# Top-31 search of a sparse attention layer: the 512 scores of a row searched as 256 pairs

## The reference, cut to what matters

```python
x = x + 0.5 * ffn(layernorm(x), ...)
x = x + attn(layernorm(x), ...)
x = x + 0.5 * ffn(layernorm(x), ...)

def attn(x, Wq, bq, Wk, bk, Wv, bv, Wo, bo):        # 16 heads of 16
    scores = einsum('bhqd,bhkd->bhqk', Q, K) / sqrt(D)          # 512 keys a row
    thresh = lax.top_k(scores, U)[0][..., -1:]                  # U = 31
    scores = where(scores < thresh, -inf, scores)
    context = einsum('bhqk,bhkd->bhqd', softmax(scores), V)
    return context @ Wo.T + bo

def layernorm(x, eps=1e-05):
    m = mean(x); v = var(x)
    return (x - m) / sqrt(v + eps)
```

## Time and profile before

| | us |
|---|---|
| median of 3 runs | 4726.12 |
| lowest and highest of them | 4723.4, 4728.99 |
| span of the profiled execution | 4725.1 |
| DVE busy | 4393.5 (93%) |
| PE busy | 4132.2 (87%) |
| ACT busy | 3967.9 (84%) |
| POOL busy | 2995.0 (63%) |

### The profile page before, as it was taken

The page is one execution under the profiler, slowest core; times in us unless marked ns, Lnnn a source line. Parts: engine busy times, 40 slices in busy tenths (PEclk is TensorE's granted clock), DMA queues, the critical chain, the costliest instruction groups (busy, mean ns, idle before and its releaser), DMA issues. The chain is left out here.

```text
span 4725.1 us, 123794 instructions
## 1 busy us (share of the span) xinstructions
PE 4132.2 (87%) x33100; PEld 3423.4 (72%) x33100; DVE 4393.5 (93%) x10203; ACT 3967.9 (84%) x10181; POOL 2995.0 (63%) x4946
## 2 busy tenths in 40 slices
PE   6778899899999889999998999998899989987777
PEld 5556777777777777777777777777777777765555
DVE  2499999999999999999999999999999999999982
ACT  2488889898898889989888998988899889888772
POOL 1445677677667767766776776677677667654440
PEclk8889999999999999999999999999999999988888
DMA  3111111121111111111111111111111111111011
GB/s 100 45 27 35 49 50 53 50 55 50 52 51 51 53 50 55 50 52 51 51 53 50 55 50 52 51 51 53 50 53 50 54 51 51 51 38 26 22 30 50
DMA packets 244162, 232.66 MB, mean 49 GB/s; under 512 B 27123, under 2 KB 176628, under 8 KB 243316
## 3 DMA queue, kind: packets, MB, share of 16 engines
q1 hardware_dynamic: 243444, 224.49, 16.6%
HBM read 214.98 MB, written 9.44 MB: 47 GB/s over the span
## 5 line engine op out<-in xcount | busy, mean ns | idle before, releaser
L1027 DVE MAX8 M<-W 128x8 f32<-128x512 f32 x2688 | 1735.2, 681 | 57.8 <-DVE W L1029 2.5
L679 PE MATMUL pQ<-wf_sb,HS 128*128 128x192 f32 x8192 | 1545.3, 345 | 81.3 <-POOL HS L419 54.1
L679 PEld LDWEIGHTS pQ<-wf_sb,HS 128*128 128x128 f32 x8192 | 1438.3, 203 | 129.5 <-issue 65.9
L1029 DVE MATCH_REPLACE8 W<-M,W 128x512 f32<-128x512 f32 x1664 | 1115.0, 676 | 0.0
L1072 POOL TENSOR_TENSOR XL<-S,LM 128x512 f32<-128x512 f32 x384 | 445.6, 1160 | 908.4 <-ACT LM L909 895.5
L698 PE MATMUL pST<-ident,S 128*128 128x128 f32 x4096 | 747.9, 283 | 15.4 <-ACT S L897 15.4
L924 ACT ACTIVATE OUT<-S,M 128x512 bf16<-128x512 f32 x1024 | 741.5, 724 | 0.0
L928 ACT ACTIVATE S<-S,M 128x512 f32<-128x512 f32 x1024 | 737.2, 720 | 0.0
L700 PE MATMUL pST<-steep,OUT 128*128 128x128 bf16 x4096 | 731.8, 222 | 0.0
L1029 DVE MATCH_REPLACE8 W<-M,S 128x512 f32<-128x512 f32 x1024 | 684.3, 676 | 0.0
L1027 DVE MAX8 M<-S 128x8 f32<-128x512 f32 x1024 | 651.5, 678 | 20.8 <-ACT S L897 10.7
(11 more groups left out here) (267 smaller groups left out, 6585.2 us busy)
## 6 DMA issues: line engine op xcount, KB each, us to landing
RB<-rows_b SPq DMA_DIRECT2D x384, 256.0 KB, 3.3
RB<-rows_a SPq DMA_DIRECT2D x384, 256.0 KB, 3.3
x_b<-in_x SPq DMA_DIRECT2D x64, 128.0 KB, 2.8
out_y<-y SPq DMA_DIRECT2D x64, 128.0 KB, 1.8
wf_sb<-in_wf SPq DMA_DIRECT2D x4, 768.0 KB, 7.4
rows_b<-rwT_b SPq DMA_DIRECT2D x64, 8.0 KB, 1.3
wof_sb<-in_wof SPq DMA_DIRECT2D x1, 1024.0 KB, 7.1
rows_a<-rwT_a SPq DMA_DIRECT2D x64, 8.0 KB, 1.4
```

The source lines that it names most:

```text
L679: mm = nc.tensor.matmul(pQ[:, 0:QKV], HS[:, k % 2, e, i, :], wf_sb[:, i, at:at + QKV], start=k + e + i == 0, stop=(k, e, i) == (3, 3, 1))
L1027: nc.vector.max(m, src[i]).then_inc(s_tk, 1)
L1029: nc.vector.match_replace(W[:, i, :], m, src[i], -BIG).then_inc(s_tk, 1)
```

## The change

**The search.** The keys are stored so that the scores matmul gives, in the first 256 columns, the difference of the scores of key j and key j + 256, and in the last 256 the score of key j + 256. For that the key tile holds three blocks (`KK`): ACT writes the two halves, POOL writes their difference after each key projection. ACT leaves each unit in three instructions of 256 columns: the second half to S, the positive part and the negative part of the difference to a new tile HL (a ring of 12). POOL adds (larger of the pair, `hi`), and makes by two subtractions the first half of S and the smaller of the pair (`lo`). DVE searches 10 passes: seven over 256 (hi: MAX8, strike, MAX8, strike; lo: MAX8, strike, MAX8, where the 16 largest of lo land beside hi) and three over 272 (hi and these 16: MAX8, strike, MAX8). All units are searched this way. The light units and all of their instructions on ACT and POOL are gone. The search of a pair of units stands two slots later than before; POOL's split stands one slot ahead of it.

**The short steps.** The mean of a layer norm is no longer scaled by a POOL instruction: ACT's square takes the factor. The gate's `RL` and `mk` go, `em` becomes two instructions. The negative maximum of the small attention comes from DVE's reduction. mixT is now written over RB2, whose load waits for the end of the matmuls that read it. Some tiles are shared by both jobs.

```diff
-SC, EV, TOP, OUTS, GAP, TR, PTE, PV, CT, CTT, CTX = 2, 3, 4, 10, 11, 16, 17, 18, 19, 20, 21
-LOW, LCOPY, LTOP, LPICK, LTH = 6, 6, 8, 9, 10
+SC, EV, SPLIT, TOP, OUTS, GAP, TR, PTE, PV, CT, CTT, CTX = 2, 3, 5, 6, 10, 11, 16, 17, 18, 19, 20, 21
...
+STEPS = (HI8, LO8, HIR, LOR, HI16, LO16, HIR2, ALL8, ALLR, ALL16)
+ORDER = [(i, k) for k in STEPS for i in range(2)]
...
-        "pT": 114, "rb2": 110, "attT": 116, "mix": 117, "y": 119, "out": 120,
+        "pT": 114, "rb2": 114, "attT": 116, "mix": 117, "y": 119, "out": 120,
...
-                ns.tensor_tensor(mixT[:], J.attT[:].unsqueeze(1).broadcast_to([P, 8, P]), RB2[:], ALU.mult
+                ns.tensor_tensor(RB2[:], attT[:].unsqueeze(1).broadcast_to([P, 8, P]), RB2[:], ALU.mult
...
-                    nc.tensor.matmul(pST[h][:], QT[r:r + 32, g // 2, g % 2, m * P:(m + 1) * P], KT[r:r + 32, g // 2, :],
+                    nc.tensor.matmul(pST[h][:], QT[r:r + 32, g // 2, g % 2, m * P:(m + 1) * P],
+                                     KK[r:r + 32, g // 2, 1:3, :].rearrange("p a j -> p (a j)"),
...
-                        nc.scalar.copy(S[:, (4 * c + h) % RING, :], pST[h][:]).then_inc(s_ev, 1)
+                        nc.scalar.copy(S[:, u % RING, HALVES:T], pST[h][:, HALVES:T])
+                        nc.scalar.activation(entry[:, 0:HALVES], pST[h][:, 0:HALVES], ACT.Relu)
+                        nc.scalar.activation(entry[:, HIL:HIL + HALVES], pST[h][:, 0:HALVES], ACT.Relu, scale=-1.0
+                                             ).then_inc(s_ev, 1)
...
-                if at := light(w, j, LCOPY):
...
-                    nc.gpsimd.tensor_tensor(XL[:, c % 2, :], S[:, r, :], LM[:, c % 2, :], ALU.subtract).then_inc(s_lx, 1)
+                for c in range(2):
+                    if at := at_proj(f"K{c}", w, j):
+                        pool.wait_ge(jobs["b"].sem["read"], fill("b", w, j) + 1)
+                        nc.gpsimd.tensor_tensor(KK[:, c, 1, :], KK[:, c, 0, :], KK[:, c, 2, :], ALU.subtract
+                                                ).then_inc(s_kd, 1)
+                if at := soon(w, j, "SPLIT", SPLIT, 2, PAIRS * NB):
+                    n, c = at
+                    for u in (2 * c, 2 * c + 1):
+                        entry = HL[:, place(w, u), :]
+                        pool.wait_ge(s_ev, w.count(SPAN, u + 1))
+                        nc.gpsimd.tensor_tensor(entry[:, 0:HALVES], S[:, u % RING, HALVES:T], entry[:, 0:HALVES], ALU.add
+                                                ).then_inc(s_hi, 1)
+                    for u in (2 * c, 2 * c + 1):
+                        entry = HL[:, place(w, u), :]
+                        pool.wait_ge(s_hi, w.count(SPAN, u + 1))
+                        nc.gpsimd.tensor_tensor(S[:, u % RING, 0:HALVES], entry[:, 0:HALVES], entry[:, HIL:HIL + HALVES],
+                                                ALU.subtract)
+                        nc.gpsimd.tensor_tensor(entry[:, HIL:HIL + HALVES], S[:, u % RING, HALVES:T],
+                                                entry[:, HIL:HIL + HALVES], ALU.subtract).then_inc(s_lo, 1)
```

More of the change, by code:

```diff
@@ L144, in earlier, with passed, place @@
     return w.count(k_all, c_all)
-def passed(w, c, k):
-    p, i = c % GANG // 2, c % 2
-    return w.count(SPAN // GANG * len(ORDER), c // GANG * len(ORDER) + ORDER.index((p, i, k)) + 1)
-def light(w, j, slot):
-    for k, u in enumerate(LIGHT):
-        if at := due(w, j, slot + u // 2 * 2, GANG, SPAN // GANG * NB):
-            n, c = at
-            return n * len(LIGHT) + k, c * len(LIGHT) + k, GANG * c + u
-    return None
+def passed(w, u, k):
+    return w.count(SPAN // 2 * len(ORDER), u // 2 * len(ORDER) + ORDER.index((u % 2, k)) + 1)
+def place(w, u):
+    return (SPAN * w.lo + u) % RINGH
 def fill(n, w, j):
@@ L388, in layer @@
                 if ends:
-                    wait(eng, g, 7 * t)
+                    wait(eng, g, 5 * t)
                 eng.wait_ge(q["repl"], t + 1)
@@ L402, in layer @@
                 eng.wait_ge(q["gate_exp"], t + 1)
-                ns.tensor_tensor(J.em[:], J.eg[:], J.mk[:], ALU.mult).then_inc(q["gate_em"], 1)
+                ns.tensor_tensor(J.ep[:], J.eg[:], J.pos[:], ALU.mult).then_inc(q["gate_em"], 1)
+                wait(eng, q["gate"], 5 * t + 5)
+                eng.wait_ge(q["gate_em"], 2 * t + 1)
+                ns.tensor_tensor(J.em[:], J.ep[:], J.fb2[:], ALU.add).then_inc(q["gate_em"], 1)
             if at := mine("rw"):
@@ L511, in ffn @@
                     held(sp, q["rw_st"], 16 * t + 16)
-                    held(sp, s_mix, earlier(w, j, MIXES.values()))
+                    held(sp, s_yd, earlier(w, j, MIXES.values()))
                     pairs = J.rows[c % 2].rearrange("(c o) t -> o c t", o=2)
@@ L623, in ffn @@
                     for k in range(4):
-                        nc.tensor.matmul(F[:, 0:D], mixT[:, k, :], wof_sb[:, k, :], start=k == 0, stop=False)
+                        nc.tensor.matmul(F[:, 0:D], RB2[:, k, :], wof_sb[:, k, :], start=k == 0, stop=False)
                 if at := tile(J, "y", w, j):
@@ L627, in ffn @@
                     for k in range(4, 8):
-                        mm = nc.tensor.matmul(F[:, 0:D], mixT[:, k, :], wof_sb[:, k, :], start=False, stop=False)
+                        mm = nc.tensor.matmul(F[:, 0:D], RB2[:, k, :], wof_sb[:, k, :], start=False, stop=False)
                     mm.then_inc(s_yd, 1)
@@ L708, in slot @@
                     if c % QUADS in (0, 2):
-                        key = "K0" if c % QUADS == 0 else "K1"
-                        sl = PROJ[key] + (c - c % QUADS) * 4
-                        pe.wait_ge(jobs["b"].sem["read"], fill("b", w, sl) + 1)
+                        pe.wait_ge(s_kd, w.count(2, c // QUADS * 2 + c % QUADS // 2 + 1))
                     wait(pe, s_ev, w.count(SPAN, 4 * c))
@@ L822, in leave @@
                     act.wait_ge(q["full"], n)
-                    nc.scalar.copy(J.rwT[:], F[0:E, 0:P]).then_inc(q["read"], 1)
+                    nc.scalar.copy(J.rwT, F[0:E, 0:P]).then_inc(q["read"], 1)
                 if at := tile(J, "qkT", w, j):
@@ L843, in leave @@
                     act.wait_ge(q["full"], n)
-                    nc.scalar.copy(J.attT[:], F[:, 0:P]).then_inc(q["read"], 1)
+                    nc.scalar.copy(attT[:], F[:, 0:P]).then_inc(q["read"], 1)
                 if at := tile(J, "y", w, j):
@@ L883, in slot @@
                     act.wait_ge(s_bop, 1)
-                    nc.scalar.copy(bo_row[:, 1, :], pO[0:1, 0:D]).then_inc(s_bo, 1)
+                    nc.scalar.copy(bo_row[:], pO[0:1, 0:D]).then_inc(s_bo, 1)
                     act.wait_ge(s_kb, 1)
-                if at := light(w, j, LOW):
-                    n, c, u = at
-                    wait(act, s_low, n)
-                    held(act, s_tk, passed(w, u, PASSES - 3))
-                    nc.scalar.activation(below[:], S[:, u % RING, :], ACT.Relu, bias=M8[:, u % RING, FOUND - 1:FOUND],
-                                         scale=-1.0).then_inc(s_lr, 1)
                 if at := soon(w, j, "EV", EV, 4, QUADS * NB):
@@ L1033, in slot @@
-                if soon(w, j, "TOP", TOP, 2, PAIRS * NB) is None:
-                    last_round(w, j)
+                        entry, m = HL[:, place(w, u), :], M8[:, u % RING, :]
+                        hi, lo, both = entry[:, 0:HALVES], entry[:, HIL:HIL + HALVES], entry[:, 0:HIL]
+                        if k == HI8:
+                            held(dve, s_hi, w.count(SPAN, u + 1))
+                        elif k == LO8:
+                            held(dve, s_lo, w.count(SPAN, u + 1))
+                        else:
+                            held(dve, s_tk, max(passed(w, u, b) for b in FOLLOWS[k])
+                                 if w.lo == w.hi else passed(w, u, max(FOLLOWS[k], key=STEPS.index)))
```

263 lines of the change are left out of this document (104 added, 159 removed).

## The result

The changed kernel takes **5075.66 us** (median of 4 runs, 5072.64 to 5078.42) where the kernel before takes 4725.61 (4 runs, 4723.40 to 4728.99) on the same chip. The ratio is 1.0741, 95% interval 1.0726 to 1.0756: it is 7.4% **slower**. The prediction had 4655 us, a range up to 4790, and 0.67 for faster. The sign was wrong, and so was the size: 421 us are missing from the sum.

A forecast was written before the change was run, and what follows sets the result against it. The bound was to move from DVE (275.6 us a batch) to POOL (274.2 with key waits). 4725.1 - 17 (middle) + 18 (POOL's waits) - 75 (ends) + 2 (first split) = 4653, so 4655 us; range 4555 to 4790.

The forecast's parts named there:

- DVE's price: DVE's search passes: 0.27 us for 256 columns, 0.285 for 272, plus 0.06 or 0.12 fixed; 3.61 us a unit, before 4.11.
- Rival 4: DVE's search: passes cost 0.42 us, so DVE stays the bound at 4.32 a unit; 4745 us, chance 0.04.
- The bound moves to POOL: Steady batch of 64 units: POOL's work reaches 266.2 us, against 239 for DVE and 253.5 for PE.
- POOL's pitch of 0.58: POOL's split and key difference: each 256-column instruction takes 0.58 us start to start, 194 of them 112.5 us a batch.
- The key waits of 4 us: POOL's key difference KK waits for ACT's key copy: 4 us each, 8 us a batch, ends 0 and 10.
- the trio: POOL's instructions pos, pick, picked, which go: 24 times a batch, 27.1 us off POOL's work.
- a wait of the bound engine is lost outright: POOL's key waits add in full to its batch as POOL is the bound: 274.2 us a batch.
- The ends bound by DVE at 3.80 a unit: Two ends with one job only, 162 units: DVE stays the bound, 616 us from 696.5, counted as -75.
- the middle: Stretch from job a's first HS piece to job b's last, 862 slots: 3693 us (-17), plus 18 for POOL's waits.
- Rival 2: POOL's split instructions don't overlap and cost 0.63 us: a batch of 284 us, 4785 us in all; chance 0.20.
- Rival 3: PE and POOL hold each other, costing 2% of the middle instead of 0.5%: +55 us, 4710; chance 0.10.
- a fuller PE: PE's granted clock, 0.95 in the steady batch and 0.85 in the ends: a fuller PE doesn't lose clock.

The follow-up runs named there:

- experiment 2: Changed kernel with one operand of each POOL split instruction made 16 columns repeated 16 times (output not the reference's): 4792.98 us, ratio 1.0143 to the kernel before.
- experiment 1: Separate small kernel timing POOL's two-input instructions by operand form, DVE idle or busy: for 256 columns 723 ns with whole f32 operands, 614 with one repeated.
- experiment 3: Changed kernel with the key difference two slots later on POOL: 4904.56 us, ratio 1.0386 to the kernel before.
- experiment 4: Changed kernel with one repeated operand in POOL's split and the key difference two slots later (output not the reference's): 4640.57 us, ratio 0.9820.
- experiment 8: Kernel of experiment 4 with DVE's row maximum two slots later for job a, one for job b: 4619.96 us, ratio 0.9777.

## Why the prediction was wrong

**DVE's price: right.** 0.35 and 0.40 us for the passes over 272, as worked out from two reductions. Rival 4 is out.

**The bound moves to POOL: right.** It is the fullest engine and has 64% of the chain that ended last.

**POOL's pitch of 0.58: the step that failed.** "I take 0.58, since the row has the same shape and inputs." The shape in the row is the output's, 128x256; ctxn multiplies by a column broadcast over 16 elements, and its code says so. The bound of 0.63 was no bound for another form either. 0.69 in place of 0.58 makes 21 us a batch, and experiment 2 gave 283 us back by the form alone. The prediction's own rule, 0.01 us for 26 us in the end, gives 286.

All three neighbours misled in the same direction, and they agreed with each other. XL and an HS piece, taken as one line, give (2.37 - 1.16) / 512 = 2.4 ns a column and no fixed part, so 0.56 for 256; but XL has a bf16 operand, and with both at whole f32 operands the line is 2.11 ns and 0.18 us (experiment 1).

The Trainium skill, "GPSIMD Engine Reference", section "Elementwise — side-by-side cycle accounting", has 4497 ns for 2048 columns. The measured line gives 0.18 + 2048 x 0.00211 = 4.50 us, so the chip agrees. Scaled in proportion it had given 0.56, since one length tells nothing of a fixed part; it was wrong for 256 columns in the same direction as the rows.

**The key waits of 4 us: mis-sized, 7.0 measured.** 14.0 a batch in place of 8 is 6.0 x 13.5 = 81 us. The two waits went wrong in different ways. In the steady loop the first is 8.4 us and the second 6.2.

The first was read in a profile in which POOL came later to the wait. The same slot as in the earlier trace rows, in the changed kernel:

```profile
2226.59 2.77 PE L650 MATMUL pQ<-wf_sb,HS 128*128 128x192 f32 x16
2227.71 2.40 POOL L398 TENSOR_TENSOR HS<-hT_b,RB 128x1024 f32<-128x1024 f32 x1
2237.70 0.81 ACT L844 ACTIVATE KK<-pFb,kbias 128x512 f32<-128x512 f32 x1
```

In the kernel before, PE began this group of matmuls at 2066.80:

```profile
2066.80 2.76 PE L679 MATMUL pQ<-wf_sb,HS 128*128 128x192 f32 x16
```

Counted from that start, POOL is through with HS after 3.52 us where it was 6.96, and the copy ends after 11.92 where it was 10.99. So 3.4 of the 4.4 us missing come from POOL being there sooner, and 0.9 from the later copy. The prediction took the work that leaves POOL's list (XL and the trio) off POOL's sum, but not out of this distance; that this work is the reason was not tested by itself.

The second wait was right as worked out, 3.7 us: with the repeated operand (experiment 2) it is 3.7 on average. At the real price of the split, POOL's mix comes later, PE stands idle before it, and the granted clock falls. The changed kernel, and behind it the clock of the mix's matmuls (the value 0.50):

```profile
2290.69 3.75 PE L594 MATMUL pFa<-wof_sb,RB 128*128 128x256 f32 x8 [3.81 <-POOL RB L411]
2294.23 3.13 PE L618 MATMUL pFb<-xnT,wqk_sb 128*128 128x512 f32 x4
```

```profile
2290.69:2294.23 3.54, 3.54 (x8) 2.83 (x9) 3.35 (x14) 0.00 (x0) 0.73 (x2) 0.50 0.03 7
```

The same matmuls with the repeated operand:

```profile
2163.27 1.97 PE L604 MATMUL pFa<-wof_sb,RB 128*128 128x256 f32 x8 [1.61 <-POOL RB L421]
2165.08 1.88 PE L628 MATMUL pFb<-xnT,wqk_sb 128*128 128x512 f32 x4
```

After 3.8 us of idle time PE runs the mix at 1.2 GHz and most of the projection behind it too (its granted clock is 0.60); they take 3.75 and 3.13 us; after 1.6 us of idle time it stays at 2.4 GHz, and they take 1.97 and 1.88. The kernel before had 1.89 and 1.88. So this part of the error is a consequence of the pitch, and the first wait is the one that was mis-sized on its own: at the pitch of 0.58 it is 9.1 us in place of 4, some 69 us in 13.5 batches.

That a wait of the bound engine is lost outright nearly held: 199 us of waits less gave 171 us (experiment 3).

**The ends bound by DVE at 3.80 a unit: half right.** DVE's work was right, its idle share was not: 104 us in place of 12. 58 of it are waits for POOL's splits, 46 of these in the first end, where the prediction allowed 2 us for the first split; 33 are job a's row maximum in the second end, a wait of 0.7 before, which DVE ran into when it had become quicker; 12 are job b's. This is +79 us. By the experiments 18 of it go with the pitch and the key waits (experiment 4) and 23 with the row maximum (experiment 8); the cause of the last 38, and with it of the long first end, stays open.

**Nothing else was large.** Of the middle's +358, 270 went with the form of the operand (3799.4 against 4069.3), the clock's part among them, and some 65 of the other 88 are the key waits that were left then (12.8 us a batch in place of 8). Rival 2 had the right sign and the right engine, with a chance of 0.20, but not the mechanism: it let the overlap fail at a duration of 0.63, while the overlap held (0.69 from start to start at a duration of 0.73) and the duration was another. Rival 3 appeared only in part, as 17 us in the middle of experiment 4. PE did lose clock, which the prediction had ruled out for a fuller PE: not by being fuller, but by standing idle for POOL.

## What to carry to other kernels

A price read from a row holds for the form of its operands, not only for its output's shape: look up in the code whether an operand is broadcast or of another type, and fit a fixed part from two lengths of the same form before scaling. When the bound moves to a new engine, cost the moved work at a form you have measured, and leave the range open upwards if you have none. Size the waits in that engine's list anew, without the work that the change takes out in front of them. When a whole time comes out right, look at its terms before you call the sum confirmed. Before giving up such a change, move something back: from 7.4% slower to 3.4% faster it took the key difference two slots later (171 us), the mix on the freed engine (DVE, at 80%; 229), the split in longer instructions (83) and the row maximum later (30).
